# Layer 0 attention: output projection of two heads summed in PSUM, in every second step

## The chip, the cores and the metric

The kernel runs on one core of one Trainium2 chip. The metric is the device time of one execution in microseconds (us); for the kernel before it is 3062.18 us, the median of three runs. A difference of 0.2% (6.1 us) is about what a measurement of this kernel can tell from none.

The engines are named as in the profile: PE (TensorE, matrix products; PEld are its weight loads), DVE (VectorE), ACT (ScalarE), POOL (GpSimd) and SP (SyncE, which here only issues transfers).

## What is computed

Two transformer layers on 1024 tokens of width 512. Layer 0 is linear attention with 32 heads of size 128 and a gated output, then a mixture of low-rank experts; layer 1 is softmax attention and an MLP. The change lies in the attention of layer 0:

```python
qkv = jax.nn.silu(hidden_states @ qkv_w.T)      # per head: q, k, v
...
kv_next = kv * block_decay + jnp.einsum('bhnd,bhne->bhde', ck * k_decay, cv)
out = intra + inter                             # per head, [tokens, 128]
...
xf = xf * jax.lax.rsqrt(jnp.mean(xf * xf, axis=-1, keepdims=True) + EPS)
normed = norm_w * xf.astype(attn.dtype)
gate = jax.nn.sigmoid(hidden_states @ gate_w.T)
return gate * normed @ out_w.T                  # sum over all 32 heads
```

The last product is a sum over the heads: each head's gated output (1024 tokens x 128) times its 128 rows of the output weights (128 x 512), added up over 32 heads. The root of the mean square is a factor per token, so the kernel applies it at the end, once.

## The kernel before

**One step for each head.** `l0_attention` writes one program for each engine. All of them walk through steps h = -1 to 32 by the function `steps`: step h does the attention of head h (`attention`), the projections of head h + 1 to queries, keys, values and gate (`project`), splits the weights of head h + 2 (`split`), and forms the output product of head h - 1 (`output`). A step has eight slots s = 0 to 7. On PE a slot holds: `scores` of half the tokens (s = 1, 3), `updates` of the states (s = 4, 5), `outputs` of half the tokens (s = 5, 7), one group of the projections (24 products of 256 columns in s = 0 to 3, `PRODUCTS` in s = 4 to 7), and last one `output_tile`. Steps 2 to 29 are a hardware loop over pairs, the others are written out. "Even" and "odd" steps below are by the head's number.

**Precision.** Each float32 product is three products of rounded parts (`three_pass`: hi*hi, hi*lo, lo*hi). So each operand is split in two: ACT copies it rounded (`..._hi`), POOL subtracts (`..._lo`). This holds for the output weights of a head, `ow_raw` to `ow_hi[b]` and `ow_lo[b]` (one raw buffer, two split ones, b = h % 2), and for its gated output, `gated` to `ga_hi[b]`, `ga_lo[b]` (in halves of 512 tokens).

**The output product.** `output_tile(h, b, t)` multiplies 128 tokens of head h with its output weights in three products of 512 columns into the bank `y_ps`; DVE's `add_output` adds the bank to the accumulator `acc` in SBUF. There is one bank, so tile t + 1 waits until tile t is added; only for the last head do two banks take turns (`y_bank`).

**The way of the keys.** The keys must be transposed to `k_T` before `scores`. DVE transposes blocks of 32 x 32 (`block_k`, s = 4 of the step before), and SP moves them through DRAM: one transfer out to `k_bounce` and, once it has landed, four back to `k_raw` (`move_k`, L383 to L391); ACT copies them to `k_T` (`copy_k`, L557, at the start of the head's step).

**SP's queue** is strictly in order, and a wait in it holds all that follows. In `load(h, b)` it issues, in this order: the K and V weights of head h, the output weights of head h - 2, `move_k(h - 2)`, the Q and gate weights of head h, the decays of head h - 1. After its loop come, written out: output weights 30, `move_k(30)`, decays, output weights 31, `move_k(31)`, then the router weights `e_raw` and the first expert weights (`in_lora_a`, four pieces) of the next stage, and the tokens `x_nat`. The load of the output weights of head h waits until those of head h - 1 are split (`wait(sp, ow_lo_done, h)`, L374), because there is one `ow_raw`.

**Between the last two heads' steps** (after step 30, "HEADS - 2") ACT and POOL also split the router and expert weights (`ew.split_high`, L666, `ew.split_low`, L523), ahead of their work for head 31.

**The end.** In step 32 PE forms the tiles of head 31; after the fourth, `mean_squares` (L812) sums the squares, POOL takes the root, and when all tiles are added, DVE and POOL add the normalised sum to the tokens and the first layer norm begins, for which PE waits.

## Time and profile before

| what | value |
|---|---|
| median of 3 runs | 3062.18 us (3061.16 to 3062.97) |
| profiled execution: its time, its span | 3054.36 us, 3052.4 us |
| granted TensorE clock, mean | 0.986 |
| attention of layer 0 | from the start to about 1113 us |
| PE busy over the span | 2927.9 us (96%) |
| DVE busy over the span | 2027.4 us (66%) |
| ACT, POOL busy over the span | 1544.3 us (51%), 1740.4 us (57%) |

The profiled execution is one execution; its time is 7.8 us below the median of the three timed runs. Durations below are from it. "Span" is from the first to the last instruction. The granted clock is given as a share of full speed: 1.00 is 2.4 GHz, 0.50 is 1.2 GHz. The end of a PE row is modelled, and consecutive products overlap in the rows: what a product costs is the distance between two starts.

### The profile page before, as it was taken

Reading aid. Unit: us, or ns where it says so; the run is one execution under the profiler, and the core shown is the slowest. Engines: PE = TensorE matmul, PEld = TensorE weight load, DVE = VectorE, ACT = ScalarE, POOL = GpSimd, SP = SyncE. Lnnn points to the kernel's source line nnn. Section 1 sums busy time; section 2 is a strip of 40 time slices with the busy share of each in tenths; the row PEclk is TensorE's granted clock in tenths of the full one; section 3 lists DMA queues with packets and bytes.
Section 4 is the critical chain, followed back from the end, with each engine's and each line's share of the span. In section 5 each row is a group of like instructions: output and inputs, shape, how many; then the busy total and the mean of one; then the engine's idle time right before and its main releaser. Section 6 shows DMA issues by size and latency. Waiting matters only on the chain. (4 is left out here: it accounts for less than half of the span.)

```text
span 3052.4 us, 57532 instructions
## 1 busy us (share of the span) xinstructions
PE 2927.9 (96%) x17440; PEld 2630.0 (86%) x17440; DVE 2027.4 (66%) x3231; ACT 1544.3 (51%) x3019; POOL 1740.4 (57%) x1300
## 2 busy tenths in 40 slices
PE   7999999999999978899999999999999999986998
PEld 6999999999999957799989899898989999975886
DVE  5555656555565556677777777777777777775555
ACT  4443443344344323566666666666666666663222
POOL 5554554455455432466665666666666666654664
PEclk9999999999999989999999999999999999998999
DMA  3222222222222220456666565665656666566541
GB/s 114 66 77 86 65 66 85 78 65 74 86 68 65 71 73 23 153 194 208 197 201 207 192 204 195 205 204 197 203 192 205 199 204 202 193 197 185 153 141 45
DMA packets 310074, 430.57 MB, mean 141 GB/s; under 512 B 30464, under 2 KB 237312, under 8 KB 309888
## 3 DMA queue, kind: packets, MB, share of 16 engines
q1 hardware_dynamic: 272336, 294.82, 32.5%
q10 hardware_dynamic: 37680, 135.02, 11.1%
q8 instruction: 31, 0.51, 0.1%
q14 instruction: 27, 0.22, 0.0%
HBM read 276.63 MB, written 153.09 MB: 141 GB/s over the span
## 5 line engine op out<-in xcount | busy, mean ns | idle before, releaser
L1588 ACT ACTIVATE b_prob<-b_s_ps,b_shift 128x1024 f32<-128x1024 f32 x256 | 285.7, 1116 | 345.9 <-DVE b_shift L1738 338.7
L82 PE MATMUL b_pj_kq<-b_w_hi,xT_hi 128*128 128x384 f32 x1008 | 351.7, 349 | 23.8 <-DVE b_nat L1714 22.5
L83 PE MATMUL b_pj_kq<-b_w_lo,xT_hi 128*128 128x384 f32 x1008 | 342.8, 340 | 0.0
L84 PE MATMUL b_pj_kq<-b_w_hi,xT_lo 128*128 128x384 f32 x1008 | 342.6, 340 | 0.0
L1744 DVE STREAM_TRANSPOSE b_blocks<-b_prob 128x1024 f32<-128x1024 f32 x256 | 317.4, 1240 | 29.0 <-ACT b_prob L1588 28.5
L489 POOL TENSOR_TENSOR a_ga_lo<-a_gated,a_ga_hi 128x512 fp32r<-128x512 f32 x64 | 112.8, 1763 | 366.7 <-ACT a_ga_hi L577 366.7
L1510 POOL TENSOR_TENSOR b_pT_lo<-b_pT_lo,b_pT_hi 128x1024 fp32r<-128x1024 f32 x128 | 304.9, 2404 | 18.7 <-ACT b_pT_hi L1577 18.6
L1510 POOL TENSOR_TENSOR pT_lo<-pT_lo,pT_hi 128x1024 fp32r<-128x1024 f32 x128 | 305.0, 2406 | 13.1 <-ACT pT_hi L1577 13.1
L1495 POOL TENSOR_TENSOR b_rstd<-b_mean_sq,power 128x4 f32<-128x4 f32 x128 | 128.8, 1007 | 320.1 <-DVE b_mean_sq L1724 313.5
L1738 DVE TENSOR_REDUCE b_shift<-b_s_ps 128x1 f32<-128x1024 f32 x256 | 307.1, 1200 | 1.7 <-PE b_s_ps L84 1.7
L82 PE MATMUL a_pj<-b_w_hi,xT_hi 128*128 128x256 f32 x1024 | 295.5, 289 | 13.2 <-DVE xT_lo L825 11.0
L84 PE MATMUL a_pj<-b_w_hi,xT_lo 128*128 128x256 f32 x1024 | 289.9, 283 | 0.0
L83 PE MATMUL a_pj<-b_w_lo,xT_hi 128*128 128x256 f32 x1024 | 289.6, 283 | 0.0
L898 DVE TENSOR_TENSOR a_kv_nat<-a_pj,a_sig 128x512 f32<-128x512 f32 x128 | 88.4, 692 | 276.2 <-ACT a_sig L603 276.2
L82 PEld LDWEIGHTS b_pj_kq<-b_w_hi,xT_hi 128*128 128x128 f32 x1008 | 190.2, 189 | 60.2 <-DVE b_nat L1714 45.2
L923 DVE TENSOR_TENSOR a_acc<-a_acc,a_y_ps 128x512 f32<-128x512 f32 x252 | 171.6, 681 | 63.7 <-PE a_y_ps L84 63.7
L1269 POOL TENSOR_TENSOR b_w_lo<-b_w_raw,b_w_hi 128x512 fp32r<-128x512 f32 x96 | 124.1, 1293 | 151.3 <-ACT b_w_hi L1262 133.8
L82 PEld LDWEIGHTS a_pj<-b_w_hi,xT_hi 128*128 128x128 f32 x1024 | 194.6, 190 | 16.1 <-issue 13.4
L82 PE MATMUL b_s_ps<-b_k_hi,b_q_hi 128*128 128x512 f32 x512 | 201.7, 394 | 6.3 <-ACT b_prob L1588 6.3
L1721 DVE TENSOR_REDUCE b_sq_sum<-b_sq 128x4 f32<-128x512 f32 x128 | 87.9, 686 | 174.0 <-ACT b_sq L1541 174.0
L84 PE MATMUL b_s_ps<-b_k_hi,b_q_lo 128*128 128x512 f32 x512 | 202.3, 395 | 0.0
L83 PE MATMUL b_s_ps<-b_k_lo,b_q_hi 128*128 128x512 f32 x512 | 201.8, 394 | 0.0
(302 smaller groups left out, 9149.3 us busy)
## 6 DMA issues: line engine op xcount, KB each, us to landing
bounce<-b_blocks ACTq DMA_DIRECT2D x256, 512.0 KB, 3.5
pT_lo<-bounce SPq DMA_DIRECT2D x512, 128.0 KB, 3.1
b_pT_lo<-bounce SPq DMA_DIRECT2D x512, 128.0 KB, 2.9
b_w_raw<-in_w SPq DMA_DIRECT2D x32, 768.0 KB, 5.8
b_w_raw<-in_w SPq DMA_DIRECT2D x95, 256.0 KB, 3.2
k_bounce<-a_k_blocks SPq DMA_DIRECT2D x32, 512.0 KB, 4.0
a_k_raw<-k_bounce SPq DMA_DIRECT2D x128, 128.0 KB, 2.9
a_w_raw<-in_w SPq DMA_DIRECT2D x32, 256.0 KB, 3.1
```

The lines of the kernel that those rows point to most:

```text
L82: pe.matmul(out, w_hi, x_hi, start=first, stop=False, skip_group_check=partial)
L83: pe.matmul(out, w_hi, x_lo, start=False, stop=False, skip_group_check=partial)
L84: return pe.matmul(out, w_lo, x_hi, start=False, stop=last, skip_group_check=partial)
L489: pool.tensor_tensor(ga_lo[b][:, cut], gated[:, cut], f(ga_hi[b][:, cut]), ALU.subtract).then_inc(ga_lo_done, 1)
L898: dve.tensor_tensor(out, pj[s % 2][:, :], sig_tmp[s % 2][:, :], ALU.mult).then_inc(silu, 1)
L923: dve.tensor_tensor(acc[:, t, :], acc[:, t, :], y_bank(h, t)[:, :], ALU.add).then_inc(y_added, 1)
L1269: pool.tensor_tensor(self.lo[b][:, :, cut], self.raw[:, :, cut], f(self.hi[b][:, :, cut]), ALU.subtract).then_inc(self.lo_done, 1)
L1495: pool.tensor_tensor(rstd[bg][:, BATCH * i:BATCH * (i + 1), :].rearrange("p t k -> p (t k)"), mean_sq[:, :, :].rearrange("p t k -> p (t k) ...
L1510: pool.tensor_tensor(lo, f(lo), f(hi), ALU.subtract).then_inc(pT_lo_done, 1)
L1588: act.activation(prob[t % 2][:, :], s_ps[t % 2][:, :], ACT.Exp, bias=shift[:, t:t + 1], accum_out=row_sum[:, t:t + 1]).then_inc(exp_done, 1)
L1738: dve.tensor_reduce(shift[:, t:t + 1], s_ps[t % 2][:, :], AX_X, ALU.max, negate=True).then_inc(shift_done, 1)
L1744: dve.transpose(blocks[t % 2][:, :, :, :].rearrange("p a m q -> p m a q"), prob[t % 2][:, :].rearrange("p (m a q) -> p m a q", a=GROUPS, q ...
```

## The change

The output products are formed in even steps only. In an even step h from 2 on, each slot takes one tile of the heads h - 2 and h - 1 together: six products into one bank, three for each head, and one addition by DVE. Odd steps have no output tile. Step 32 (after the last head) takes heads 30 and 31, with two banks in turn. What was 256 additions is now 128; the number of products is the same.

Since both halves of the double buffers `ga_..[b]` and `ow_..[b]` are now read in an even step, they come free only in its course: the split of the output weights of an even head moves from slot 3 to the end of the step, on ACT and on POOL, and waits there for the step's last tile; the split of the gated halves in even steps waits for tiles of the same step (`outputs_done`). In `load`, SP's transfer of the output weights goes behind `move_k`. The written-out end of SP's queue is not touched.

```diff
         def y_bank(h, t):
-            return pj[0] if isinstance(h, int) and h == HEADS - 1 and t % 2 else y_ps
+            return pj[0] if isinstance(h, int) and h == HEADS - 2 and t % 2 else y_ps
+        def outputs_done(h, b, half):
+            return 4 * h - 4 + (0 if b else 4 * half)
...
             def one(h):
-                step(h, h % 2, 0 <= h < HEADS, h + 1 < HEADS, h >= 1, h + 2 < HEADS)
+                step(h, h % 2, 0 <= h < HEADS, h + 1 < HEADS, h >= 2 and h % 2 == 0, h + 2 < HEADS)
-            for h in (-1, 0, 1):
+            for h in (-1, 0, 1, 2, 3):
                 one(h)
-            with eng.Fori(2, HEADS - 3, 2) as h:
+            with eng.Fori(4, HEADS - 3, 2) as h:
                 step(h, 0, True, True, True, True)
-                step(h + 1, 1, True, True, True, True)
+                step(h + 1, 1, True, True, False, True)
...
                 load_weights(h, 1)
+                move_k(h - 2)
                 load_output_weights(h - 2)
-                move_k(h - 2)
...
+            def output_weights_low(h, b):
+                pool.wait_ge(ow_in, 16 * (h + 1))
+                pool.wait_ge(ow_hi_done, h + 1)
+                wait(pool, y_done, outputs_done(h, b, 1))
+                pool.tensor_tensor(ow_lo[b][:, :], ow_raw[:, :], f(ow_hi[b][:, :]), ALU.subtract).then_inc(ow_lo_done, 1)
...
-                    if attention and s == 3:
...
+                    if attention and s == 3 and b:
+                        output_weights_low(h, b)
...
                 if attention:
                     half_out(h, b, 1)
+                if attention and not b:
+                    output_weights_low(h, b)
                 if isinstance(h, int) and h == HEADS - 2:
                     ew.split_low(pool, 0)
...
             def gated_hi(h, b, j):
                 cut = slice(j * HALF, (j + 1) * HALF)
                 act.wait_ge(gated_done, 2 * h + j + 1)
-                wait(act, y_done, NT * (h - 1))
+                wait(act, y_done, outputs_done(h, b, j))
...
                 if attention:
                     gated_hi(h, b, 1)
+                if attention and not b:
+                    output_weights_high(h, b)
                 if isinstance(h, int) and h == HEADS - 2:
                     ew.split_high(act, 0)
...
-                three_pass(pe, y_bank(h, t)[:, :], ga_hi[b][:, cut], ga_lo[b][:, cut], ow_hi[b][:, :], ow_lo[b][:, :],
-                           True, True).then_inc(y_done, 1)
+                for b in range(2):
+                    last = three_pass(pe, y_bank(h, t)[:, :], ga_hi[b][:, cut], ga_lo[b][:, cut], ow_hi[b][:, :],
+                                      ow_lo[b][:, :], b == 0, b == 1)
+                last.then_inc(y_done, 1)
...
                     if output:
-                        output_tile(h - 1, 1 - b, s)
+                        output_tile(h - 2, s)
```

**SP, in its loop.** Each row is an instruction of SP's queue with its line in the program; `a_ow_raw` are the output weights, `k_bounce` and `a_k_raw` the two parts of `move_k`; in brackets is what it waits for. Before:

```order
L365 DMA b_w_raw<-in_w 128x4x128
L375 ISA [waits a_ow_lo_done]
L375 DMA a_ow_raw<-in_ow 128x512
L387 DMA k_bounce<-a_k_blocks 128x1024 [waits a_k_blocked]
L389 ISA
L391 DMA a_k_raw<-k_bounce 32x4x256 [waits a_k_moved]
L391 DMA a_k_raw<-k_bounce 32x4x256 x3
```

With the change (its lines are numbered anew):

```order
L371 DMA b_w_raw<-in_w 128x4x128
L393 DMA k_bounce<-a_k_blocks 128x1024 [waits a_k_blocked]
L395 ISA
L397 DMA a_k_raw<-k_bounce 32x4x256 [waits a_k_moved]
L397 DMA a_k_raw<-k_bounce 32x4x256 x3
L381 ISA [waits a_ow_lo_done]
L381 DMA a_ow_raw<-in_ow 128x512
```

The pair has changed places: the transfer that waits for `ow_lo_done` now stands behind the keys.

**SP, behind its loop.** From the decays of head 31 on, with the change:

```order
L387 DMA a_decay<-in_decay 128x258 [waits a_attn]
L381 DMA a_ow_raw<-in_ow 128x512 [waits a_ow_lo_done]
L393 DMA k_bounce<-a_k_blocks 128x1024 [waits a_k_blocked]
L397 DMA a_k_raw<-k_bounce 32x4x256 [waits a_k_moved]
L397 DMA a_k_raw<-k_bounce 32x4x256 x3
L1017 DMA e_raw<-in_router 128x32
L428 DMA b_w_raw<-in_lora_a 128x4x128 [waits a_w_lo_done] x3
L428 DMA a_w_raw<-in_lora_a 128x4x128 [waits a_w_lo_done]
L431 DMA x_nat<-in_x 128x8x512 [waits a_proj]
```

These rows stand in the same order before the change (L381, L375, L387, L391, L997, L422, L425 there). Here the output weights of head 31 still stand ahead of `k_bounce` of head 31.

**POOL, in the step of head 30.** `a_ow_lo` is the split of its output weights, which counts `ow_lo_done` up; `a_ga_lo` and `a_sq_sum` are the two halves of its output; `e_lo` belongs to the router and expert weights. Before:

```order
L501 TENSOR_TENSOR a_ow_lo<-a_ow_raw,a_ow_hi 128x512 [waits a_y_done,a_ow_hi_done,a_ow_in]
L489 TENSOR_TENSOR a_ga_lo<-a_gated,a_ga_hi 128x512 [waits a_y_done,a_gated_done,a_ga_hi_done]
L493 TENSOR_TENSOR a_sq_sum<-a_sq_sum,a_squares 128x512 [waits a_sq_added,a_squared]
L489 TENSOR_TENSOR a_ga_lo<-a_gated,a_ga_hi 128x512 [waits a_y_done,a_gated_done,a_ga_hi_done]
L493 TENSOR_TENSOR a_sq_sum<-a_sq_sum,a_squares 128x512 [waits a_sq_added,a_squared]
L1006 TENSOR_TENSOR e_lo<-e_raw,e_hi 128x32 [waits e_w_hi,e_w_in0]
L523 TENSOR_TENSOR e_lo<-b_w_raw,e_hi 128x4x128 [waits e_w_hi,a_w_in0,a_proj]
```

With the change:

```order
L495 TENSOR_TENSOR a_ga_lo<-a_gated,a_ga_hi 128x512 [waits a_y_done,a_gated_done,a_ga_hi_done]
L499 TENSOR_TENSOR a_sq_sum<-a_sq_sum,a_squares 128x512 [waits a_sq_added,a_squared]
L495 TENSOR_TENSOR a_ga_lo<-a_gated,a_ga_hi 128x512 [waits a_y_done,a_gated_done,a_ga_hi_done]
L499 TENSOR_TENSOR a_sq_sum<-a_sq_sum,a_squares 128x512 [waits a_sq_added,a_squared]
L506 TENSOR_TENSOR a_ow_lo<-a_ow_raw,a_ow_hi 128x512 [waits a_y_done,a_ow_hi_done,a_ow_in]
L1026 TENSOR_TENSOR e_lo<-e_raw,e_hi 128x32 [waits e_w_hi,e_w_in0]
L534 TENSOR_TENSOR e_lo<-b_w_raw,e_hi 128x4x128 [waits e_w_hi,a_w_in0,a_proj]
```

The split of the output weights of head 30 has moved from ahead of both halves to behind them.

**ACT, from the end of step 30 to the first copy of the keys of head 31**, with the change:

```order
L594 ACTIVATE a_ga_hi<-a_gated 128x512 [waits a_y_done,a_gated_done]
L588 ACTIVATE a_ow_hi<-a_ow_raw 128x512 [waits a_y_done,a_ow_in]
L1021 ACTIVATE e_hi<-e_raw 128x32 [waits e_w_in0]
L683 ACTIVATE e_hi<-b_w_raw 128x4x128 [waits a_w_in0,a_proj]
L683 ACTIVATE e_hi<-b_w_raw 128x4x128 [waits a_w_in1]
L683 ACTIVATE e_hi<-b_w_raw 128x4x128 [waits a_w_in2]
L683 ACTIVATE e_hi<-a_w_raw 128x4x128 [waits a_w_in2]
L568 ACTIVATE a_k_T<-a_k_raw 128x4x4x32 [waits a_scored,a_k_moved]
```

Before, the same rows stood there without the second one, `a_ow_hi`, which came in slot 3.

## Rows read from the trace of the kernel before

**Rows 1.** Windows of core 0: start:end and length, busy us, PEclk, DMA share, GB/s.

```profile
47.40:50.40 3.00, 2.92 (x13) 2.93 (x14) 1.38 (x2) 1.63 (x4) 1.28 (x1) 0.50 0.00 0
120.00:1060.00 940.00, 940.00 (x6239) 859.12 (x6239) 547.39 (x899) 378.31 (x701) 487.33 (x451) 1.00 0.23 74
...
1082.60:1092.40 9.80, 8.85 (x34) 7.45 (x34) 3.44 (x5) 2.29 (x5) 7.12 (x7) 0.54 0.28 106
1125.50:1132.50 7.00, 6.25 (x21) 5.13 (x22) 2.53 (x4) 1.79 (x3) 0.14 (x1) 0.50 0.70 262
```

**Rows 2.** Waits of PE from 13 to 120 us: total, times, longest.

```profile
PE a_s_ps L749 <- ACT a_k_T L557: 6.2, 1, 6.2
```

**Rows 3.** Groups by line: DVE's additions; busy us, mean ns, idle before.

```profile
L923 DVE TENSOR_TENSOR a_acc<-a_acc,a_y_ps 128x512 f32<-128x512 f32 x252 | 171.6, 681 | 63.7 <-PE a_y_ps L84 63.7
```

**Rows 4.** Timeline of PE in a step of the loop: start, us, engine, line, operation.

```profile
453.26 0.39 PE L82 MATMUL a_y_ps<-a_ow_hi,a_ga_hi 128*128 128x512 f32 x1
...
453.95 1.05 PE L749 MATMUL a_s_ps<-a_q_T,a_k_T 128*128 128x128 f32 x8
```

**Rows 5.** Timeline of ACT in the same step.

```profile
450.46 0.62 ACT L591 ACTIVATE a_s_hi<-a_s_raw 128x512 fp32r<-128x512 f32 x1
...
451.29 0.62 ACT L557 ACTIVATE a_k_T<-a_k_raw 128x512 f32<-128x512 f32 x1
```

**Rows 6.** Timeline of POOL at the start of the same step.

```profile
447.22 0.75 POOL L455 TENSOR_TENSOR a_s_raw<-b_w_raw 128x256 f32<-128x256 f32 x1
...
448.62 0.75 POOL L458 TENSOR_TENSOR a_s_raw<-a_s_raw,a_w_raw 128x256 f32<-128x256 f32 x1
```

**Rows 7.** Timeline of SP's queue, step 30.

```profile
1065.01 0.33 SPq L387 DMA_DIRECT2D k_bounce<-a_k_blocks  x1
1067.68 1.75 SPq L391 DMA_DIRECT2D a_k_raw<-k_bounce  x4
...
1071.92 0.63 SPq L422 DMA_DIRECT2D a_w_raw<-in_lora_a  x1
```

**Rows 8.** The four transfers of expert weights, L422.

```profile
DMA to landing us min/median/max: 3.5/3.9/4.9
```

**Rows 9.** Timeline of ACT ahead of head 31.

```profile
1081.49 0.61 ACT L666 ACTIVATE e_hi<-a_w_raw 128x512 fp32r<-128x512 f32 x1
1082.01 0.61 ACT L557 ACTIVATE a_k_T<-a_k_raw 128x512 f32<-128x512 f32 x1
```

**Rows 10.** Timeline of POOL, end of step 30 and step 31.

```profile
1082.09 1.27 POOL L493 TENSOR_TENSOR a_sq_sum<-a_sq_sum,a_squares 128x512 f32<-128x512 f32 x1
...
1088.44 1.27 POOL L501 TENSOR_TENSOR a_ow_lo<-a_ow_raw,a_ow_hi 128x512 fp32r<-128x512 f32 x1
```

**Rows 11.** Timeline of PE, DVE and ACT in the step of head 31.

```profile
1082.68 2.08 PE L749 MATMUL a_s_ps<-a_q_T,a_k_T 128*128 128x128 f32 x8 [1.74 <-ACT a_k_T L557]
...
1084.79 0.69 DVE L867 TENSOR_TENSOR a_s_masked<-a_s_ps,a_decay 128x512 f32<-128x512 f32 x1 [3.13 <-PE a_s_ps L749]
...
1088.32 1.91 PE L749 MATMUL a_s_ps<-a_q_T,a_k_T 128*128 128x128 f32 x8
...
1097.26 0.75 DVE L891 SCALAR_TENSOR_TENSOR a_gated<-a_o_ps,a_norm_sb,a_gate_T 128x512 f32<-128x512 f32 x1 [1.08 <-ACT a_squares L571]
...
1099.52 0.39 PE L769 MATMUL a_o_ps<-a_s_masked,a_kv_nat 128*128 128x128 f32 x2
...
1101.50 0.60 ACT L571 ACTIVATE a_squares<-a_o_ps 128x512 f32<-128x512 f32 x1 [2.83 <-PE a_o_ps L774]
```

**Rows 12.** Timeline of SP's queue, the keys of head 0.

```profile
37.77 0.42 SPq L387 DMA_DIRECT2D k_bounce<-a_k_blocks  x1
42.41 1.75 SPq L391 DMA_DIRECT2D a_k_raw<-k_bounce  x4
```

**Rows 13.** Timeline of PE and DVE, step 32: mean squares, last addition.

```profile
1106.91 1.84 PE L812 MATMUL a_s_ps<-a_ones,a_sq_sum 128*128 128x1 f32 x16
...
1112.10 0.69 DVE L923 TENSOR_TENSOR a_acc<-a_acc,a_pj 128x512 f32<-128x512 f32 x1
```

More of the change, by code:

```diff
@@ L487, in half_out @@
                 pool.wait_ge(gated_done, 2 * h + j + 1)
-                wait(pool, y_done, NT * (h - 1))
+                wait(pool, y_done, outputs_done(h, b, j))
                 pool.tensor_tensor(ga_lo[b][:, cut], gated[:, cut], f(ga_hi[b][:, cut]),
@@ L571, in square, with output_weights_high @@
                 act.activation(squares[:, cut], o_ps[:, :], ACT.Square).then_inc(squared, 1)
+            def output_weights_high(h, b):
+                act.wait_ge(ow_in, 16 * (h + 1))
+                wait(act, y_done, outputs_done(h, b, 1))
+                act.activation(ow_hi[b][:, :], ow_raw[:, :], ACT.Copy).then_inc(ow_hi_done, 1)
             def gated_hi(h, b, j):
@@ L633, in step @@
                             decay_k(h, b, s // 2)
-                        if s == 3:
-                            act.wait_ge(ow_in, 16 * (h + 1))
-                            wait(act, y_done, NT * (h - 1))
-                            act.activation(ow_hi[b][:, :], ow_raw[:, :], ACT.Copy).then_inc(ow_hi_done, 1)
+                        if s == 3 and b:
+                            output_weights_high(h, b)
                         if s in (5, 7):
@@ L660, in step @@
                     gated_hi(h, b, 1)
+                if attention and not b:
+                    output_weights_high(h, b)
                 if isinstance(h, int) and h == HEADS - 2:
@@ L671, in _ @@
             for t in range(0, NT, 2):
-                act.wait_ge(y_added, NT * (HEADS - 1) + t + 1)
+                act.wait_ge(y_added, NT * (HEADS // 2 - 1) + t + 1)
                 act.activation(acc[:, t, :], acc[:, t, :], ACT.Copy, scale=rms[:, t:t + 1]).then_inc(normalised, 1)
@@ L775, in outputs, with output_tile @@
                 last.then_inc(attn, 1)
-            def output_tile(h, b, t):
-                pe.wait_ge(ga_lo_done, 2 * h + t // CH + 1)
-                pe.wait_ge(ow_lo_done, h + 1)
-                wait(pe, y_added, NT * h + (t - 1 if t and y_bank(h, 1) is not y_ps else t))
+            def output_tile(h, t):
+                pe.wait_ge(ga_lo_done, 2 * h + 2 + t // CH + 1)
+                pe.wait_ge(ow_lo_done, h + 2)
+                wait(pe, y_added, NT // 2 * h + (t - 1 if t and y_bank(h, 1) is not y_ps else t))
                 cut = slice(t * P, (t + 1) * P)
-                three_pass(pe, y_bank(h, t)[:, :], ga_hi[b][:, cut], ga_lo[b][:, cut], ow_hi[b][:, :], ow_lo[b][:, :],
-                           True, True).then_inc(y_done, 1)
+                for b in range(2):
+                    last = three_pass(pe, y_bank(h, t)[:, :], ga_hi[b][:, cut], ga_lo[b][:, cut], ow_hi[b][:, :],
+                                      ow_lo[b][:, :], b == 0, b == 1)
+                last.then_inc(y_done, 1)
             def step(h, b, attention, project, output, split):
@@ L920, in add_output @@
             def add_output(h, t):
-                dve.wait_ge(y_done, NT * h + t + 1)
-                wait(dve, y_added, NT * (h - 1) + t + 1)
+                dve.wait_ge(y_done, NT // 2 * h + t + 1)
+                wait(dve, y_added, NT // 2 * h - NT + t + 1)
                 dve.tensor_tensor(acc[:, t, :], acc[:, t, :], y_bank(h, t)[:, :], ALU.add).then_inc(y_added, 1)
@@ L951, in step @@
                     if output:
-                        add_output(h - 1, s)
+                        add_output(h - 2, s)
                     if isinstance(h, int) and h == HEADS and s == CH - 1:
@@ L961, in _ @@
             dve.wait_ge(const_in, 32)
-            dve.wait_ge(y_added, NT * HEADS)
+            dve.wait_ge(y_added, NT * HEADS // 2)
             for t in range(0, NT, 2):
```

5 lines of the change are left out of this document (removed).

## The prediction

> **What bounds the kernel now.** I first read the windows [rows 1]. From 120 to 1060 us, the loop over the heads, PE is busy for 940.00 of 940.00 us at full clock (1.00). So in the loop nothing but PE's own work sets the time. DVE is busy for 547 us of them, POOL for 487. Then I asked what the change takes away: 128 of DVE's 256 additions of 681 ns [rows 3], some 87 us. DVE has that time to spare in the loop, and PE does the same products as before. The addition therefore frees nothing that PE waits for, and the gain in the loop is zero. What is left are the two ends, where PE does wait: at the start, 6.2 us for the first copy of the keys [rows 2], and at the end, from 1077.7 us on, where a window shows it at half clock (0.54) after a wait [rows 1]. Last I followed each queue whose order moves into these ends.
>
> **The loop.** A tile costs PE 453.95 - 453.26 = 0.69 us [rows 4]; an even step gets 8 more, an odd step 8 fewer, in sum none. The question is what an odd step, now shorter, runs into. The tightest place I find is the second half of `scores`. At the end of the even step ahead of it POOL now also splits the output weights, 1.27 us (the row at 1088.44) [rows 10], and ACT and POOL wait for a tile 7 of double length, which I put at 0.1 us. So the sums of the weights that POOL starts at 447.22 start some 1.4 us later, and the third, at 448.62 for 0.75 us, ends at 450.8 instead of 449.4 [rows 6]. ACT's conversion at 450.46 waits for this sum: it comes 0.35 us later, and the copy of the keys behind it, at 451.29 for 0.62 us, ends at 452.3 [rows 5]. PE wanted it at 453.95; now four tiles ahead of that place are gone and one has double length less one, so it wants it 2 x 0.69 = 1.4 us earlier, at 452.6 [rows 4]. 0.3 us are left. I take 0.5 us of stalls in all. The bounds: zero, and 0.3 us in each of 14 odd steps, 4.2 us. The other waits that the change adds (the gated halves on tiles of the same step, the output weights of odd heads loaded only when those of the even one are split) I put at nothing: ACT and POOL idle for about half of the loop or more [rows 1], and the parts are not wanted before the next even step. What this would cost without that cover is in the bound of the stalls.
>
> **The start.** The transfer of the keys of head 0 is issued at 37.77, behind that of the output weights, and the four back at 42.41 [rows 12]; PE waits 6.2 us for what follows. With the pair exchanged it is issued one issue earlier, about 0.5 us. The way out took 4.64 us here, and 1067.68 - 1065.01 = 2.67 us in step 30, with nothing issued just ahead of it [rows 7], so it may be up to 2.0 us shorter too: the gain lies between 0.5 and 2.5 us; I take 1.1, nearer to the low end, since the V weights still go out just ahead. Against it: steps 0 and 1 have no tile at all to cover ACT's and POOL's longer end of step 0, which I price as two small waits of 0.3 and 0.4 us (bounds 0 and 1.5). Net -0.4 us.
>
> **The end, and its queue.** This is where the sum is made. Before, the output weights of head 30 were split in slot 3 of step 30, long before `move_k(31)`; SP issued `k_bounce` at 1065.01 [rows 7]. Now they are split last in that step. SP's next transfer, the output weights of head 31, waits for that count, and behind it stand `move_k(31)`, the router and the expert weights; the exchange was made in `load` and not here. The steps:
> - POOL's last work in step 30 ended at 1082.09 + 1.27 = 1083.4 [rows 10]. PE reaches that point one tile earlier than before (it has formed 8h - 2 tiles instead of 8h - 1), so 1082.8. The added split of 1.27 us ends at 1084.1.
> - SP issues the output weights (0.5 us) and then `k_bounce` at 1084.6: 19.6 us late.
> - All that follows it takes as long as before: from `k_bounce` at 1065.01 to the last piece of expert weights at 1071.92 [rows 7], and at most 4.9 us to its landing [rows 8], so 1076.8; this was hidden, since ACT wanted it at 1081.49 [rows 9]. Now it lands at 1096.4.
> - ACT's order is: that conversion, then the keys. From its start at 1081.49 to PE's scores at 1082.68 were 1.2 us [rows 9, 11]. So the scores of head 31 begin at 1097.6, not 1082.68. PE stands still for some 19 us.
>
> **From the scores to the last output of head 31.** Before, 1101.50 - 1082.68 = 18.8 us [rows 11]. Without tiles PE loses three pieces: the second scores could start when the first are masked, at 1084.79 + 0.69 = 1085.5 instead of 1088.32 (2.8 us); the tile behind them, twice 0.69 us at half clock (1.4 us); and the second outputs could start when the first half is gated, 1097.26 + 0.75 = 1098.0 instead of 1099.52 (1.5 us). That leaves 13.1 us. The clock is the open part. After the wait before 1082.68 it was 0.54 for 9.8 us, after the 12.7 us ahead of 1125.5 it was 0.50 for 7.0 us, after the 6.2 us at the start 0.50 for 3.0 us [rows 1]. With 7 to 10 us after 1097.6 the scores (2.08 and 1.91 us, as shown) and also the first updates are at half clock, about 0.9 us more: 14.0 us, and the last output ends at 1111.6, 10.1 us later than before.
>
> The Trainium skill ("TensorE: Matmul & The Clock Gate", section "What's actually happening") has the low clock as the state after idling and says that activity ends it. By that rule dense work would end it soon, as in the window from 47.4; the window from 1082.6, with gaps between the products, shows it lasting three times as long, and this stage will have gaps of the same kind, so I go by the latter. With the former, 3.0 us, the second scores and the updates would run at full clock and the sum would be 1.9 us less. If on the other hand the gaps keep the clock low until step 32, updates, outputs (twice 1.9 us more) and some tiles are longer by 4 to 7 us.
>
> **Step 32.** It now has 8 tiles of 1.38 us and the mean squares, 1.8 us [rows 13], then the last addition, 0.9 us with its wait: 13.8 us after the last output. Before, the last addition ended at 1112.10 + 0.69, 11.3 us after it. That is 2.5 us more, up to 3 with the wait for the first split half; 2.7. What follows is the same work as before and is only moved.
>
> **The sum.** -0.4 at the start, +0.5 in the loop, +10.1 to the last output, +2.7 in step 32: +12.9 us. The profiled execution would take 3067.3 us instead of 3054.4. The same difference on the median of 3062.18 gives 3075.1 us.
>
> **The rivals.**
> - *The queue does not hold the keys* (the order shown is right, but the wait ends early or ACT is not behind it). Then the scores start at 1082.6 as before, the last output comes 14.0 us later, at 1096.6, 4.9 us earlier than before, and with +2.7 and +0.1 the sum is -2.1: 3060 us, within 0.2%. Against it: the rows of the queues leave no way around. Chance 0.05; another 0.03 that it comes to nothing by causes that I do not see.
> - *Odd steps stall by more.* If POOL's chain is 0.5 us longer than I reckon, each of 14 steps loses 0.2 to 0.7 us; at 0.5 us the sum is 7 us higher, 3082 us. For it: only 0.3 us are left. Chance 0.10, slower.
> - *The clock stays low* through the gaps of the last step: +4 to +7 us, 3079 to 3082 us. Chance 0.10, slower.
> - *Faster: the products get denser in the loop.* If DVE's additions, which read PSUM while PE writes it, slow the products, half of them gone could shorten the loop. It decides only if PE gains more than 12.9 + 6.1 = 19 us of the 940 us in the loop, 2%; the time would then be below 3056 us. Against it: there is no gap in the loop's window, and PE would have to lose 19 of the 87 us of additions taken away, over a fifth of the time that each one lasts, of which no row shows a sign. Chance 0.03.
> - The forecast has the remaining 0.69.
>
> **Numbers.** Likeliest 3075.1. Low end: clock back early (-1.9), the whole gain at the start and no waits behind it (-2.5 instead of -0.4), no stalls (-0.5), step 32 at its least (-0.2) makes +8.2, 3070.4; high end: clock low through the last step (+7) or stalls in the loop (+3.7 to +7), 3084. The range is 3069 to 3084, which leaves out the rivals on the other side and the worst of both upper ones. Faster by over 0.2% 0.03, within 0.2% 0.09, slower by over 0.2% 0.88.
>
> **What would show it.** In the profile of the changed kernel: DVE's additions 128, busy down by some 87 us, and PE in the loop still without waits (or with up to 0.3 us on `scores` in odd steps). SP's `k_bounce` for head 31 stands right behind a transfer of output weights, some 20 us later than its neighbours' place in the step, and just after POOL's last split in step 30. ACT waits for DMA there, for about 15 us, on the router and expert weights, and PE waits for ACT's copy of the keys with an idle time of about 19 us; the granted clock is 0.5 behind it. The step behind the last output takes 13.8 us to the last addition. The forecast is wrong if that wait on SP is short, if PE finds something to do in the 19 us, or if odd steps show a wait for each head.

## The result, and the profile after

The changed kernel takes 3074.74 us (median of 5 runs, 3073.01 to 3075.84), the kernel before 3061.16 us in the same comparison (5 runs, 3056.76 to 3062.97): ratio 1.0048, 95% interval 1.0033 to 1.0062, which is 10 to 19 us. The forecast was 3075.1 us. The profiled execution took 3073.01 us, span 3071.2 us, mean clock 0.984.

Windows of the changed kernel: start:end, length, busy us of each engine, PEclk, DMA share, GB/s.

```profile
120.00:1060.00 940.00, 940.00 (x6229) 857.70 (x6228) 489.40 (x784) 377.18 (x700) 481.44 (x448) 1.00 0.24 74
1082.00:1102.00 20.00, 0.00 (x0) 0.00 (x0) 1.76 (x2) 3.98 (x8) 7.93 (x7) 0.61 0.54 153
1102.00:1113.00 11.00, 8.13 (x35) 7.60 (x36) 3.32 (x8) 2.59 (x5) 3.20 (x3) 0.50 0.33 128
1086.30:1113.60 27.30, 8.73 (x37) 8.20 (x38) 3.76 (x9) 5.42 (x10) 7.53 (x7) 0.50 0.53 164
```

The loop stands as in [rows 1]: PE busy for all of its time, DVE 58 us less. Then a hole of 20 us in which PE does nothing, and 11 us at half clock behind it; the clock had fallen in the hole, by 1086.3. Waits of PE in the changed kernel, from 1060 to 1150 us:

```profile
PE a_s_ps L766 <- ACT a_k_T L568: 20.5, 1, 20.5
PE e_t_ps L180 <- PEq L238: 11.5, 1, 11.5
PE a_u_ps L774 <- DVE a_state L901: 1.6, 1, 1.6
PE a_o_ps L786 <- DVE a_gated L911: 1.6, 1, 1.6
```

The first has taken the place of 1.7 us in [rows 11]; six waits for DVE's additions to free a bank (5.5 us before, from the last slot of step 30 to step 32) are gone. What holds PE is found on the queues. SP's queue of the changed kernel, against [rows 7]:

```profile
1087.35 0.35 SPq L381 DMA_DIRECT2D a_ow_raw<-in_ow  x1
1087.75 0.43 SPq L393 DMA_DIRECT2D k_bounce<-a_k_blocks  x1
1091.82 1.75 SPq L397 DMA_DIRECT2D a_k_raw<-k_bounce  x4
...
1096.06 0.63 SPq L428 DMA_DIRECT2D a_w_raw<-in_lora_a  x1
```

`k_bounce` is issued at 1087.75, was 1065.01. It stands behind the transfer of the output weights, and this one behind POOL's split. POOL and then ACT in the changed kernel, against [rows 9, 10]:

```profile
1086.06 1.26 POOL L506 TENSOR_TENSOR a_ow_lo<-a_ow_raw,a_ow_hi 128x512 fp32r<-128x512 f32 x1
```

```profile
1082.54 0.61 ACT L588 ACTIVATE a_ow_hi<-a_ow_raw 128x512 fp32r<-128x512 f32 x1
1096.50 0.23 ACT L1021 ACTIVATE e_hi<-e_raw 128x32 fp32r<-128x32 f32 x1 [13.35 <-DMA e_raw<-in_router]
...
1101.19 0.61 ACT L683 ACTIVATE e_hi<-a_w_raw 128x512 fp32r<-128x512 f32 x1
1101.71 0.61 ACT L568 ACTIVATE a_k_T<-a_k_raw 128x512 f32<-128x512 f32 x1
```

The split ends at 1087.3; SP issues at 1087.35. ACT waits 13.35 us for the router weights, then three times more for expert weights (0.56, 0.20 and 1.91 us); its last conversion starts at 1101.19, the keys at 1101.71. Then PE and ACT in the step of head 31, against [rows 11]:

```profile
1102.37 2.08 PE L766 MATMUL a_s_ps<-a_q_T,a_k_T 128*128 128x128 f32 x8 [20.47 <-ACT a_k_T L568]
...
1105.33 2.05 PE L766 MATMUL a_s_ps<-a_q_T,a_k_T 128*128 128x128 f32 x8 [0.87 <-DVE a_s_masked L887]
...
1110.70 1.62 PE L774 MATMUL a_u_ps<-a_kv_nat,a_k_dec 128*128 128x128 f32 x6 [1.63 <-DVE a_state L901]
...
1116.11 0.46 PE L786 MATMUL a_o_ps<-a_s_masked,a_kv_nat 128*128 128x128 f32 x2 [1.56 <-DVE a_gated L911]
...
1118.17 0.60 ACT L582 ACTIVATE a_squares<-a_o_ps 128x512 f32<-128x512 f32 x1 [1.54 <-PE a_o_ps L791]
```

15.8 us from the scores to the last output (18.8 in the trace of before). "The last output" is here and below the start of ACT's second row on `a_squares`, which waits for it. And the end of step 32, DVE and PE, against [rows 13]:

```profile
1131.09 0.69 DVE L943 TENSOR_TENSOR a_acc<-a_acc,a_pj 128x512 f32<-128x512 f32 x1 [0.67 <-PE a_pj L84]
1131.91 0.75 DVE L984 SCALAR_TENSOR_TENSOR x_nat<-a_acc,a_rms,x_nat 128x512 f32<-128x512 f32 x1
...
1142.59 1.94 PE L180 MATMUL e_t_ps<-ident,x_nat 128*128 128x128 f32 x8 [11.53 <-PEq L238]
```

### The profile page after: what moved, and what is told of

Its sections match the earlier page's. It is cut to its first block and busy times, and to the rows that moved or that the text cites. A ratio compares the mean times of both kernels' runs of the same rounds, so it can differ in the third digit from the quotient of the medians.

```text
span 3071.2 us, 56804 instructions
## 1 busy us (share of the span) xinstructions
PE 2929.1 (95%) x17440; PEld 2630.4 (86%) x17440; DVE 1959.3 (64%) x3103; ACT 1544.4 (50%) x3019; POOL 1737.2 (57%) x1300
## 5 line engine op out<-in xcount | busy, mean ns | idle before, releaser
L1530 POOL TENSOR_TENSOR pT_lo<-pT_lo,pT_hi 128x1024 fp32r<-128x1024 f32 x128 | 305.1, 2406 | 13.6 <-ACT pT_hi L1597 13.6
L82 PE MATMUL a_pj<-b_w_hi,xT_hi 128*128 128x256 f32 x1024 | 296.0, 289 | 14.4 <-DVE xT_lo L845 11.3
L83 PEld LDWEIGHTS a_pj<-b_w_lo,xT_hi 128*128 128x128 f32 x1024 | 195.6, 191 | 2.1
```

The costliest lines, as they stand in the source:

```text
L82: pe.matmul(out, w_hi, x_hi, start=first, stop=False, skip_group_check=partial)
L83: pe.matmul(out, w_hi, x_lo, start=False, stop=False, skip_group_check=partial)
L1530: pool.tensor_tensor(lo, f(lo), f(hi), ALU.subtract).then_inc(pT_lo_done, 1)
```

## The experiments

Each was timed in five rounds, together with the kernel before on the same chip. The three groups ran on three chips; before had medians of 3059.48 us (e1 to e4), 3058.87 us (e5 to e8) and 3059.16 us (e9, e10) there. A ratio is to the kernel before in the same group, with its 95% interval; across groups, ratios are compared and not times. Line numbers differ by a few from kernel to kernel. Where the total can't tell two theories apart, the stretch of the trace that the run is about does.

### e1: the keys ahead of the output weights behind the loop too

```diff
-            load_output_weights(HEADS - 1)
             move_k(HEADS - 1)
+            load_output_weights(HEADS - 1)
```

> The changed kernel, with the keys of head 31 moved ahead of its output weights at the end of SP's queue; the router and expert weights stay behind the output weights. Theory A (everything behind the held transfer counts, because ACT converts the expert weights before it copies the keys): the keys land early, but the expert weights still wait for POOL's last split of step 30 (1087.3); only the way of the keys, 0.4 + 4.07 + 1.75 us, drops out ahead of them, so the scores of head 31 start about 6 us earlier than at 1102.4, at 1096, and the time falls by about 6 us to 3068. Theory B (the keys alone are what PE waits for): the scores start some 19 us earlier, at 1083, and the time falls below 3058.

Measured: 3067.84 us, ratio 1.0032 (1.0020 to 1.0044). SP's queue, and PE's wait, in e1:

```profile
1065.45 0.34 SPq L393 DMA_DIRECT2D k_bounce<-a_k_blocks  x1
1068.13 1.75 SPq L397 DMA_DIRECT2D a_k_raw<-k_bounce  x4
1087.55 0.35 SPq L381 DMA_DIRECT2D a_ow_raw<-in_ow  x1
...
1090.40 0.63 SPq L428 DMA_DIRECT2D a_w_raw<-in_lora_a  x1
```

```profile
PE a_s_ps L766 <- ACT a_k_T L568: 16.2, 1, 16.2
```

The keys are in time again (1065.45), and PE still waits 16.2 us: ACT's order puts the router and expert weights ahead of the keys, and their transfers are still behind the held one. That is theory A, but the scores start at 1098.28, 4.1 us earlier and not 6. ACT waits 3.21 us for the third piece of expert weights here, 1.91 us in the changed kernel. Only 4 of the 20 us are the keys' own way; undoing the order of this pair alone does not undo the slowdown.

### e2: the output weights of head 31 behind everything but the tokens

```diff
-            load_output_weights(HEADS - 1)
             move_k(HEADS - 1)
...
+            load_output_weights(HEADS - 1)
```

(the line now stands behind the expert weights, ahead of `x_nat`)

> The changed kernel, with the output weights of head 31 issued last, behind the keys, the router and the expert weights. Theory A (the slowdown is this wait in SP's queue): ACT finds everything there, the scores of head 31 start at about 1085.5, the last output is 13 to 14 us behind them (18.8 before, as no tiles stand between), and the whole is 16 to 19 us below the changed kernel in the profile's last stage: about 3058 to 3062, no difference to the kernel before that can be measured. Rival (the step without tiles and step 32 with twice as many are what costs): the scores start early, but the layer norm behind the attention still begins 10 us or more later than before, and the time stays above 3067.

Measured: 3056.91 us, ratio 0.9996 (0.9987 to 1.0005). SP's queue, and PE's wait, in e2:

```profile
1065.72 0.34 SPq L393 DMA_DIRECT2D k_bounce<-a_k_blocks  x1
...
1072.63 0.63 SPq L427 DMA_DIRECT2D a_w_raw<-in_lora_a  x1
1087.85 0.35 SPq L381 DMA_DIRECT2D a_ow_raw<-in_ow  x1
```

```profile
PE a_s_ps L766 <- ACT a_k_T L568: 4.0, 1, 4.0
```

One line moved, and the whole slowdown is gone, as theory A said. Its 13 to 14 us from the scores to the last output were too few: it is 15.3 us (1086.40 to 1101.75), with the granted clock at 0.50 for 10 us of it. The summed tiles themselves neither cost nor gain anything that the total can tell: e2, with them, and e3, without, lie within 1 us. In the traces they move work. Seven tiles fewer stand ahead of the scores of head 4, and the eight tiles behind head 31 are double.

### e3: the exchange in `load` alone, on the kernel before

```diff
-                load_output_weights(h - 2)
                 move_k(h - 2)
+                load_output_weights(h - 2)
```

> The kernel before, with only the exchange in SP's loop (keys ahead of the output weights). If the way of the keys of head 0 gets shorter once nothing large stands between: PE's first wait for the keys falls from 6.2 us to between 3.7 and 5.7 us, and the time by the same 0.5 to 2.5 us, which is within the noise. If only the place in the queue counts: 0.5 us less. The loop is unchanged at 33.48 us a head.

Measured: 3057.64 us, ratio 0.9995 (0.9986 to 1.0004). PE's first wait for the keys:

```profile
PE a_s_ps L749 <- ACT a_k_T L557: 5.1, 1, 5.1
```

5.1 us where before had 6.2 [rows 2]: the exchange takes 1.1 us off that wait. The way out to DRAM took 4.60 us (4.64 before), so it did not get shorter; the place in the queue alone was to give 0.5 us, and what gives the rest is not shown. In the time it is not seen, and the first scores of head 4 do not start earlier by it (181.36 us, 178.08 before).

### e4: additions of 16 columns

```diff
-            def add_output(h, t):
+            def add_output(h, t, width=D):
...
-                        add_output(h - 1, s)
+                        add_output(h - 1, s, 16 if not b and not isinstance(h, int) else D)
```

(`width` is the number of columns that DVE adds)

> The kernel before, with DVE adding only 16 of 512 columns for the odd heads of the hardware loop (112 additions), so that part of the sum is left out: DVE's work goes down by about 65 us and nothing else changes. If additions cost PE nothing, as argued: 33.48 us a head in the loop as before, and the same time within 0.1%. Rival (an addition that reads PSUM slows the products): less than 33.48 us a head, down to 32.8 if a fifth of each addition's time is PE's.

Measured: 3058.49 us, ratio 1.0000 (0.9991 to 1.0010). Two heads take 66.96 us in the loop, to the hundredth as before. Shortening 112 of DVE's additions changes nothing for PE; the rival by which the products get denser without them is refuted.

### e5: the keys ahead of the conversions on ACT and POOL

```diff
@@ e2, ACT and POOL
-                if isinstance(h, int) and h == HEADS - 2:
-                    ew.split_high(act, 0)
...
+                    if isinstance(h, int) and h == HEADS - 1 and s == 4:
+                        ew.split_high(act, 0)
...
```

> The kernel of e2_weights_last, with ACT's and POOL's conversions of the router's and the expert weights moved from the end of step 30 to slot 4 of step 31, so that the copy of the keys of head 31 stands directly behind the split of the output weights on ACT. Theory A (what PE waits for ahead of the last scores is ACT's order, wherever a conversion stands ahead of the keys): the wait falls from 4.0 us to about 1.8 us; if the clock then drops for less time, the 15.3 us from the last scores to the last output become 13 to 14. Together 2 to 5 us less than e2_weights_last: 3052 to 3055 us, and below the kernel before by 0.1 to 0.2%. Rival B (the conversions only move into the last step, where ACT and POOL are wanted for the weights and gated halves): the wait falls but the stretch from scores to last output grows by about as much (four conversions of some 1 us each), and the time stays at that of e2_weights_last.

Measured: 3054.45 us, ratio 0.9984 (0.9974 to 0.9993). PE in e5:

```profile
1082.18 1.16 PE L767 MATMUL a_s_ps<-a_q_T,a_k_T 128*128 128x128 f32 x8 [1.82 <-ACT a_k_T L568]
1084.21 1.55 PE L767 MATMUL a_s_ps<-a_q_T,a_k_T 128*128 128x128 f32 x8 [0.88 <-DVE a_s_masked L888]
...
1089.09 0.91 PE L775 MATMUL a_u_ps<-a_kv_nat,a_k_dec 128*128 128x128 f32 x6 [1.62 <-DVE a_state L902]
```

The wait fell from 4.0 to 1.8 us, and the stretch to the last output from 15.3 to 13.0 us. The first scores run at full clock (1.16 us for eight products) in e2 too. What differs is how long the clock is low behind them: 10 us in e2, here from 1084.9 to 1088.1. Both numbers are those of theory A, and so is the time. But rival B's cost is there as well, one step later. POOL's conversions now stand ahead of its split of the gated halves, PE waits for that split in step 32, and the clock is low there a second time:

```profile
1097.08 0.50 PE L82 MATMUL a_y_ps<-a_ow_hi,a_ga_hi 128*128 128x512 f32 x1 [1.94 <-POOL a_ga_lo L495]
```

```profile
1098.50:1101.70 3.20, 3.20 (x9) 2.46 (x8) 0.85 (x2) 0.00 (x0) 2.25 (x2) 0.50 0.01 3
```

From the last output to the last addition it takes 17.3 us, 13.6 in e2. Of the 4.5 us gained up to the last output, 3.7 go again.

### e6: the last two heads' tiles taken singly

```diff
@@ e5, PE; DVE's additions alike
-                        output_tile(h - 2, s)
+                        if isinstance(h, int) and h >= HEADS - 1:
+                            output_tile(HEADS - 2, s, (h - HEADS + 1,))
+                        else:
+                            output_tile(h - 2, s)
...
```

> The kernel of e5_keys_before_conversions, with the tiles of the last two heads taken singly as in the kernel before: head 30's in step 31 (three matmuls a tile), head 31's in step 32, on two banks. It tells the term of step 32 and of the gaps in step 31. Theory A (tiles in step 31 fill gaps of PE that are there anyway and take their 8 x 0.69 us out of step 32): step 32 gets some 2.3 us shorter and the stretch from scores to last output longer by 0 to 3 us, net 0 to -3 us against e5. Rival B (what DVE adds singly meets POOL's additions ahead of the layer norm again, 1.7 us for the first piece instead of 0.75): the 2.3 us come back as 1.9 there, net about 0 or +1 us.

Measured: 3062.79 us, ratio 1.0014 (1.0005 to 1.0023), some 8 us above e5. Neither theory's time holds. PE in e6:

```profile
1087.95 0.77 PE L82 MATMUL a_y_ps<-a_ow_hi,a_ga_hi 128*128 128x512 f32 x1 [5.53 <-POOL a_ow_lo L506]
...
1092.91 0.47 PE L82 MATMUL a_y_ps<-a_ow_hi,a_ga_hi 128*128 128x512 f32 x1 [0.87 <-POOL a_ow_lo L506]
```

The first tile of head 30 waits 5.5 us in slot 0 of step 31 for the split of its output weights, which the change has moved to the end of step 30, and the scores stand behind it in PE's order. Neither theory had counted when that operand is ready. The run does tell the term of step 32. With single tiles the last addition ends 11.3 us behind the last output, as in before; it is 13.6 us with the summed ones in the changed kernel and in e2. And DVE's first addition to the tokens is slow again, as rival B said:

```profile
1116.97 1.69 DVE L993 SCALAR_TENSOR_TENSOR x_nat<-a_acc,a_rms,x_nat 128x512 f32<-128x512 f32 x1
```

### e7: spare products in the 20 us wait

```diff
+                        if isinstance(h, int) and h == HEADS - 1 and s == 0:
+                            pe.wait_ge(combined, NC * HEADS)
+                            for n in range(84):
+                                pe.matmul(c_ps[n % 2][:, :], sh.xT_hi[:, n % KB, 0:P], sh.xT_hi[:, n % KB, 0:HALF],
+                                          start=True, stop=True)
```

> The changed kernel, and 84 spare products of 512 columns on PE (transposed input by itself into two unused banks, read by nobody) in the 20.5 us in which it waits for the keys of head 31. It prices the clock in the forecast's stretch from the last scores to the last output. Theory A (the low clock after the wait made 15.8 us of the 13.1 that I worked out at full clock): the scores still begin some 54 us after the last step-30 work at about 1102.4, the granted clock behind them is 1.00, the stretch is 13 to 13.5 us, and the time is 2.3 to 2.8 us below the changed kernel: 3072 us. Rival B (the stretch is long by waits between engines, not by the clock): clock 1.00 but the stretch stays at 15 to 16 us and the time is unchanged, 3074 to 3075 us.

Measured: 3074.24 us, ratio 1.0048 (1.0035 to 1.0062). Windows of e7:

```profile
1082.00:1101.00 19.00, 19.00 (x85) 15.42 (x83) 1.82 (x2) 2.72 (x6) 7.50 (x6) 1.00 0.48 146
1102.00:1113.00 11.00, 7.45 (x34) 6.92 (x35) 3.14 (x8) 3.26 (x6) 3.76 (x3) 0.57 0.33 123
```

PE was busy at clock 1.00 for 19 us, then idle for 2.0 us, and the clock fell in the sparse stretch all the same (0.57 over 11 us), while the first scores ran. The stretch took 15.3 us. Theory A's condition, a clock of 1.00, did not come about, so the run does not price the clock and does not decide between the two. What it shows is that the low clock is not left over from the long wait: here a gap of 2.0 us ahead of the scores and gaps of 0.9 and 1.6 us behind them came before it.

### e8: the kernel before, with both orders mended

```diff
@@ before, SP
-                load_output_weights(h - 2)
                 move_k(h - 2)
+                load_output_weights(h - 2)
@@ before, ACT and POOL: router and expert weights as in e5
```

> The kernel before, with the exchange of keys and output weights in load (as in the change) and the conversions of router and expert weights in slot 4 of step 31 as in e5_keys_before_conversions; additions and tiles as before. Theory A (the wait ahead of the last scores is ACT's order in this kernel too; in the profile of before PE waited 1.7 us and 1.4 us there and the clock was 0.54 for 9.8 us): 2 to 3 us less than the kernel before, 3056 to 3058 us. Rival B (the conversions meet the last step's own work): no change, 3059 us. Beside e5 it tells whether the summed tiles are worth anything once both queues' ends are in order: A for that says e5 and e8 are within 2 us of each other.

Measured: 3052.48 us, ratio 0.9980 (0.9971 to 0.9989). A window of e8, against the third of [rows 1]:

```profile
1082.60:1092.40 9.80, 7.83 (x44) 6.16 (x45) 7.42 (x13) 5.28 (x11) 9.44 (x8) 1.00 0.58 203
```

Clock 1.00 where it was 0.54. From the scores at 1083.76 to the last output at 1099.21 it takes 15.5 us, 18.8 before. But the trace of before is not typical here. e3 and e4 leave this step as it was, and their clock is low for a shorter time. In e4 the stretch took 16.69 us at a clock of 0.91; here it is in before, e3 and e8:

```profile
1082.68:1101.50 18.82, 15.69 (x79) 13.25 (x80) 8.45 (x16) 3.43 (x6) 9.54 (x9) 0.76 0.14 54
1085.95:1102.60 16.65, 13.60 (x79) 11.24 (x80) 8.45 (x16) 3.45 (x6) 9.58 (x9) 0.90 0.17 64
1083.76:1099.21 15.45, 12.41 (x80) 10.26 (x79) 9.34 (x18) 5.34 (x11) 11.51 (x10) 1.00 0.30 115
```

So the clock gives 1.2 us against e3 and e4, and 3.4 us against the one trace of before; the wait of 1.7 us ahead of the scores is gone besides. That is theory A's mechanism and its 2 to 3 us. The median is 6.4 us below before (3.4 to 8.9 by the ratio's interval), more than it said, and the traces do not show where the rest is. e5 and e8 lie within 2 us of each other, as A said; PE's first transposes of the next stage start at 1123.30 us in e5 and at 1123.22 in e8.

### e9: spare products in all of PE's gaps of step 31

```diff
@@ e7
-                        if isinstance(h, int) and h == HEADS - 1 and s == 0:
+                        if isinstance(h, int) and h == HEADS - 1 and s in (0, 3, 5, 7):
...
-                            for n in range(84):
+                            for n in range({0: 90, 3: 3, 5: 6, 7: 6}[s]):
```

> The changed kernel with spare products of 512 columns (transposed input by itself into unused banks, read by nobody) in all of PE's gaps of step 31: 90 ahead of the scores (20.9 us at 0.232 us each, where e7 had 84 and left 2.0 us idle, behind which the clock fell to 0.50 all the same), 3 ahead of the second scores (a gap of 0.9 us), 6 ahead of the second updates (1.6 us) and 6 ahead of the second outputs (1.6 us). Theory A (the gaps, not the 20 us wait, brought the low clock, and the clock makes 15.8 us of the 13.1 worked out at full clock): the granted clock stays at 1.00 from 1082 us on, scores begin at 1102.4 to 1103, the last output ends 13 to 13.5 us later, and the time is 2 to 2.5 us below the changed kernel: 3072 us. Rival B (the granted clock does not matter there, the other engines' chain sets the stretch): clock 1.00 and the stretch still 15 us or more, 3074 us.

Measured: 3073.04 us (3072.39 to 3074.96), ratio 1.0051 (1.0037 to 1.0065). Window, then PE and ACT of e9:

```profile
1102.00:1113.00 11.00, 9.64 (x63) 7.77 (x61) 4.25 (x10) 4.51 (x8) 3.77 (x3) 1.00 0.38 141
```

```profile
1103.70 1.16 PE L766 MATMUL a_s_ps<-a_q_T,a_k_T 128*128 128x128 f32 x8 [0.96 <-ACT a_k_T L568]
...
1105.73 1.13 PE L766 MATMUL a_s_ps<-a_q_T,a_k_T 128*128 128x128 f32 x8 [0.18 <-DVE a_s_masked L892]
...
1109.38 0.91 PE L774 MATMUL a_u_ps<-a_kv_nat,a_k_dec 128*128 128x128 f32 x6 [0.23 <-DVE a_state L906]
...
1115.47 0.60 ACT L582 ACTIVATE a_squares<-a_o_ps 128x512 f32<-128x512 f32 x1 [1.54 <-PE a_o_ps L791]
```

The clock held, and the stretch took 11.8 us, from 1103.70 to 1115.47, against 15.8. So the low clock costs 4.0 us there; rival B falls. It is also less than theory A's 13 to 13.5 us, which came from my 13.1 us: I had called them worked out at full clock, but they hold the scores at half clock. In the trace PE's first transposes of the next stage come 2.7 us earlier than in the changed kernel (1139.93), and not 4.0, since the scores start 1.3 us later here: ACT waits 2.90 us for the third piece of expert weights, not 1.91. In the total it does not stand out: the ratio's interval is 9 us wide, and a later stretch that no edit here touches (from PE's wait of 4.0 us near 1210 us to its wait of 8.7 us near 2808 us) took 1599.5 us in this trace and 1596.5 us in that of the changed kernel.

### e10: the conversions alone

```diff
@@ e8
-                move_k(h - 2)
                 load_output_weights(h - 2)
+                move_k(h - 2)
```

> The kernel of e8_before_keys_first without the exchange in load: the kernel before with nothing changed but the place of the conversions of the router and expert weights (slot 4 of step 31). Theory A (the gain of e8, 0.2% over before, is from the end: with the keys ahead of these conversions PE has scores to do at once and the granted clock stays at 1.00 through the last step): ratio 0.998 as e8, within 1 us of it, 3052 to 3054 us. Rival B (the gain needs the exchange at the start too, or is that exchange's in a better run): the ratio lies at 0.999 or above, 3056 us or more.

Measured: 3054.90 us, ratio 0.9986 (0.9977 to 0.9995). Its interval overlaps that of e8, and in the last step its trace is that of e8 to 0.1 us (scores to last output 15.5 us, clock 1.00). It lies between the two theories' numbers. The gain, 4.3 us (1.5 to 7.0 by the ratio's interval), is there without the exchange; whether the exchange adds to it can't be told.

## Why the prediction was right

The time, the place and the mechanism were right; four terms were mis-sized and one was not foreseen, and they partly cancel. That the median came within 0.4 us of the forecast is luck: the interval of the difference is 9 us wide, and single terms are off by up to 1.9 us. "Single" kernels below are before, e3, e4, e8, e10; "summed" are the changed kernel, e1, e2, e5, e6, e7, e9. The table is read from the starts of the `scores` products in each trace.

| | single (5) | summed (7) |
|---|---|---|
| first scores of head 0 | 47.48 to 50.59 | 46.78 to 48.89 |
| first scores of head 4, mean | 180.44 (178.08 to 181.84) | 175.37 (173.80 to 175.87) |
| from head 4 to head 30 | 870.48 in each | 871.60 to 871.61 |

- **Loop, gain of the additions: zero.** Right. 128 additions are gone (3231 DVE instructions to 3103), DVE's busy time fell by 68 us (the 87 us are rows, and rows overlap), PE's window is still 940.00 of 940.00, and e4 shows the length of the additions to be free.
- **Loop, +0.5 us of stalls.** It is +1.1 us from head 4 to head 30, in every trace of the summed tiles, so within my bounds, but not by my mechanism: PE waits neither for the keys nor for anything else. The same products take 0.09 us longer in each 67 us. Why, no run settles; that one is luck too.
- **Start, -0.4 us.** The profiled pair suggests the opposite: seven tiles fewer stand ahead of head 4 (4.8 us), and the changed kernel is only 2.7 us earlier there, so +2.1 us. But single kernels vary by 3.8 us at this place, and before is the earliest of them. By the means, 180.44 - 4.83 = 175.61 against 175.37: -0.2. A wait shorter by 1.1 us is there (e3), but the way out was hardly shorter (4.1 to 4.6 us in the traces with the exchange, 4.6 to 4.8 in those without); of the two small waits against it the trace shows one of 0.2 us. What else there is lies below the variation of the runs.
- **End, `k_bounce` at 1084.6.** 1087.75, but all of step 30 stands 3.2 us later in the profiled pair (2.1 us from the start and 1.1 from the loop, above), so the term was right. e1 and e2 show its two parts: of the 20.5 us, 4.3 are the keys' own, 12.2 the weights ahead of them on ACT, and 4.0 were left in e2 (2.2 of these are ACT's conversions ahead of the keys, by e5).
- **"All that follows takes as long as before."** Wrong by 1.4 us: from `k_bounce` to the four transfers back 4.07 us, not 2.67 [rows 7]. In e1 and e2, where nothing is issued just ahead, it takes 2.68 us; in the changed kernel the output weights stand 0.4 us ahead. I had used just this difference for the start, and did not carry it to the end. And two conversions, not one, come after the last landing that ACT waits for (0.5 us), which itself is 0.3 us quicker than my 4.9.
- **From the scores to the last output, 14.0 us.** 15.8 us. The chain is as forecast; the clock is the term that was too small. I added 0.9 us for it to a sum whose scores were already at half clock; at full clock the stretch takes 11.8 us (e9), so the low clock costs 4.0 us. It was low from 1086.3 on, in the wait, and stayed so for 11 us behind it, with gaps of 0.9 and 1.6 us between the products; with these gaps filled it was not low at all (e9). My 18.8 us to start from were themselves a slow case, 16.7 us in e3 and e4. And the wait ahead of 1125.5 that I gave as 12.7 us is 13.5 us in PE's own row; no term rests on it. The rule of the Trainium skill that I weighed ("TensorE: Matmul & The Clock Gate", "What's actually happening": activity ends the low clock) would have made it shorter. In this trace 11 us of sparse products did not end it, and in e7 it fell although 19 us of dense work stood ahead. e9 agrees with the rule: with dense work the clock stays at 1.00.
- **Step 32, +2.7 us.** +2.3 (13.6 us to the end of the last addition, forecast 13.8; 11.3 with single tiles in e6).
- **"What follows is only moved."** Wrong by -1.9 us. DVE in the kernel before, then POOL, and POOL in the changed kernel:

```profile
1112.92 1.71 DVE L964 SCALAR_TENSOR_TENSOR x_nat<-a_acc,a_rms,x_nat 128x512 f32<-128x512 f32 x1
...
1115.83 1.69 DVE L964 SCALAR_TENSOR_TENSOR x_nat<-a_acc,a_rms,x_nat 128x512 f32<-128x512 f32 x1
```

```profile
1111.58 5.39 POOL L532 TENSOR_TENSOR x_nat<-x_nat,a_acc 128x512 f32<-128x512 f32 x4 [0.90 <-ACT a_acc L673]
```

```profile
1128.29 5.50 POOL L543 TENSOR_TENSOR x_nat<-x_nat,a_acc 128x512 f32<-128x512 f32 x4 [0.90 <-ACT a_acc L690]
```

Before, POOL starts its additions to the tokens 1.3 us ahead of DVE's, and two of DVE's take 1.7 us; now POOL is 3.6 us ahead, and they take 0.75 and 0.72. The Trainium skill ("SBUF — State Buffer", "SBUF: two separate sides") says that VectorE with two SBUF inputs and GpSimd exclude each other on a shared pair of ports. The rows agree: before, DVE's row starts while POOL's second addition runs and lasts beyond its end (1114.1). In the changed kernel DVE's first row still falls into POOL's, but only near the end of POOL's third addition, and stays short; POOL's fourth takes the time instead, and its last two take 2.99 us against 2.54 for the first two:

```profile
1130.79 2.99 POOL L543 TENSOR_TENSOR x_nat<-x_nat,a_acc 128x512 f32<-128x512 f32 x2
```

All six traces with single tiles at the end (e6 is one) have DVE's 1.7 us, all six with summed ones 0.75. That POOL's head start is what makes the difference was not tried by itself.

The sum by these sizes: -0.2 + 1.1 + 13.4 to the last output + 2.3 - 1.9 = +14.7 us, in the 10 to 19 us measured (13.4 is 1118.17 - 1101.50 less the 3.2 us by which the profiled pair differs already ahead of it). It starts from the trace of before; with the step of head 31 as in e3 and e4 it is some 17 us, also within. The rivals: "the queue does not hold the keys" is out by the trace, "odd steps stall" too (no wait), "the clock stays low" came part of the way (1.8 us over the forecast, where it had +4 to +7; the clock is back before the last outputs), and "denser products" is out by e4.

**A version faster than both** is e8, 3052.48 us: 0.2% below before (0.11% to 0.29%), and 0.7% below the changed kernel. The 0.7% compare two ratios to before, of different groups. It has none of the summed tiles. e5, with them, has 3054.45 us; their intervals overlap.

## What to carry to other kernels

When an order is changed inside a loop, look for the copies of that order that are written out behind it: here one line left in its old place cost some 16 us (e2 against the changed kernel, by their ratios), in a change that by itself brings nothing, and it did so through transfers that had nothing to do with it, since an in-order queue hands a wait on to all that follows. Ask of the last step of a loop in what order its first operand comes, and put work for the next stage behind it, but not ahead of what the last step itself needs (e5). Freeing an engine that had time to spare gained nothing here, with 128 of its instructions gone. And a single trace of the kernel before can hold a slow case: compare a stretch with other runs that leave it untouched.

## What the hardware showed that I had not expected

- PE's granted clock fell to half during a stretch with gaps of 0.9 and 1.6 us, also when 19 us of dense work and only a 2.0 us pause came before (e7). In the step of head 31 it was low for 11 us in the changed kernel, for some 3 us in e5, and with the gaps filled not at all (e9). Over this one stretch it costs up to 4.0 us. But gaps of this size do not always bring it: in e8 PE pauses for 1.38 us ahead of the last tile before the scores and for 0.87, 0.71 and 1.46 us behind them, with tiles in between, and the clock stays at 1.00. No run here tells the rule.
- The same step at the same order of work had the clock at 0.76 on average in the trace of before and at 0.90 and 0.91 in e3 and e4, and took 18.8, 16.7 and 16.7 us.
- The way out of the keys to DRAM takes 2.67 us with nothing issued just ahead, 3.8 to 4.1 us with another transfer issued 0.4 us ahead in the same queue (e7, e9, changed kernel), and 4.1 to 4.8 us at the start.
- Products in the loop run at 67.05 us for two heads with summed tiles and at 66.96 with single ones, in seven and five traces, at the same count of products and without a wait of PE. No run shows why.
- Untouched stretches vary from run to run: 3.8 us up to head 4, 3.0 us between 1210 and 2808 us. A single profiled pair would have told a wrong story of the start.
